# A ring of eight column copies in the token mix of a MetaFormer block, with two small instructions moved

## What is computed

```python
x = x + conv_ref(_ln_c(x), ...)         # Fourier layers, attention over the 32 tokens of a batch
t = _to_tokens(x)
t = t + ffn_ref(_ln_t(t), ...)          # a product, a batch norm, and a scan y = sigmoid(Wx + y @ V.T)
# inside conv_ref, of normed tokens:
k, q, v = (fno_layer(tokens_norm, w, skip_w, skip_b, size) for each of key, query, value)
attn = softmax(q k^T / scale) v                      # 16 heads, tokens by tokens
attn = fno_layer(attn, proj_w, proj_skip_w, ...)     # back to one channel
attn = instance_norm(attn + tokens)
m = instance_norm(attn)
m = gelu(instance_norm(spectral_conv(m, mixer_w1)) + skip1 * m)
m = instance_norm(spectral_conv(m, mixer_w2)) + skip2 * m
out = instance_norm(m) + attn
```

## Time and profile before

| | us |
|---|---|
| median of 3 runs | 428.48 (423.45 to 432.25) |
| the profiled execution | 428.99 |
| its span, first to last instruction | 427.2 |
| TensorE busy | 351.0 (82%) |
| VectorE busy | 338.9 (79%) |
| ScalarE busy | 229.8 (54%) |
| GpSimd busy | 219.3 (51%) |
| mean granted TensorE clock | 0.955 |

### The profile page before, as it was taken

One profiled execution on the slowest core, in us unless ns is written; L12 is line 12 of the kernel. 1 busy time (PEld: TensorE's weight loads), 2 busy tenths in 40 slices (PEclk: granted clock), 3 DMA queues, 4 the chain that ended last, 5 costly groups with the idle time before them and its releaser, 6 DMA issues.

```text
span 427.2 us, 7193 instructions
## 1 busy us (share of the span) xinstructions
PE 351.0 (82%) x2415; PEld 273.8 (64%) x2415; DVE 338.9 (79%) x994; ACT 229.8 (54%) x511; POOL 219.3 (51%) x265
## 2 busy tenths in 40 slices
PE   0289979998893999998999599768888889999940
PEld 0289965975451899987889558434444447767940
DVE  2999762768896958469998787999999649999990
ACT  0498851801023687445565025688776869898000
POOL 1289960041003797599961109888884779600000
PEclk9999999999998899989999869999999989999985
DMA  8999997998505000089898740222234200000997
GB/s 217 241 291 319 290 282 172 220 277 367 198 4 195 1 0 3 0 100 160 106 170 103 93 62 2 100 102 99 100 127 172 101 1 0 2 0 19 280 287 206
DMA packets 62999, 58.37 MB, mean 137 GB/s; under 512 B 5792, under 2 KB 55376, under 8 KB 60912
## 3 DMA queue, kind: packets, MB, share of 16 engines
q1 hardware_dynamic: 43232, 49.20, 38.6%
q0 software_dynamic: 16512, 8.39, 16.1%
q10 hardware_dynamic: 3216, 0.30, 0.7%
HBM read 38.84 MB, written 16.94 MB: 131 GB/s over the span
## 4 chain that ended last, share of the span: by engine, by line
PE 42%; DVE 28%; POOL 11%; issue 4%; DMA 3%; ACTq 3%; ACT 3%; SPq 2%; DVEq 0%; POOLq 0%
PE PS L640 36%; POOL BIG L571 8%; PE PS L644 6%; DVE SML L1204 6%; DVE BIG L1344 5%; DVE BIG L1536 4%; DVE BIG L1553 3%; ACTq L1007 2%; SPq L513 2%; DMA BIG<-BIG 2%; DMA BIG<-xn_rows 2%; DVE BIG L1436 1%; POOL BIG L590 1%; DVE BIG L1432 1%; POOL BIG L619 1%
## 5 line engine op out<-in xcount | busy, mean ns | idle before, releaser
L640 PE MATMUL PS<-CST,BIG 128*128 128x128 f32 (+6 forms) x994 | 123.4, 313 | 14.6 <-ACT BIG L1012 5.1
L640 PEld LDWEIGHTS PS<-CST,BIG 128*128 128x128 f32 (+1 forms) x994 | 110.9, 194 | 30.5 <-DVE BIG L1536 9.9
L1204 DVE BATCH_NORM_STATS2 SML<-BIG 128x6 f32<-128x128 f32 x256 | 53.5, 280 | 5.8 <-DMA BIG<-in_x 4.5
L640 PE MATMUL PS<-BIG 128*128 128x128 f32 (+2 forms) x450 | 53.8, 368 | 4.6 <-DVE BIG L1344 4.1
L644 PEld LDWEIGHTS PS<-CST,BIG 128*128 128x128 f32 (+1 forms) x326 | 41.4, 182 | 19.3 <-issue 13.7
L590 POOL COPY BIG<-BIG 128x512 f32<-128x512 f32 x24 | 30.5, 1320 | 39.7 <-DMA BIG<-xn_rows 36.6
L644 PE MATMUL PS<-CST,BIG 128*128 128x128 f32 (+1 forms) x326 | 48.6, 290 | 2.7 <-ACT SML L402 1.7
L640 PEld LDWEIGHTS PS<-BIG 128*128 128x128 f32 (+2 forms) x450 | 40.5, 168 | 15.4 <-issue 7.6
L640 PE MATMUL PS<-BIG,SML 128*128 128x256 f32 (+4 forms) x230 | 48.9, 415 | 0.0
L402 ACT ACTIVATE BIG<-PS 128x512 f32<-128x512 f32 (+3 forms) x59 | 32.1, 568 | 26.0 <-PE PS L640 21.0
L1577 DVE SCALAR_TENSOR_TENSOR PS<-BIG,SML,PS 128x256 f32<-128x256 f32 x92 | 41.2, 490 | 5.2 <-PE PS L640 5.1
(11 more groups left out here) (218 smaller groups left out, 496.6 us busy)
## 6 DMA issues: line engine op xcount, KB each, us to landing
xn_rows<-BIG SPq DMA_DIRECT2D x8, 1024.0 KB, 9.0
BIG<-xn_rows SPq DMA_DIRECT2D x8, 1024.0 KB, 8.8
BIG<-in_x POOLq DMA_DIRECT2D x8, 1024.0 KB, 10.9
BIG<-rs_rows SPq DMA_DIRECT2D x8, 1024.0 KB, 4.7
out_x<-BIG SPq DMA_DIRECT2D x32, 256.0 KB, 3.8
BIG<-wy_rows SPq DMA_DIRECT2D x16, 192.0 KB, 6.5
BIG<-BIG SPq DMA_DIRECT2D x16, 128.0 KB, 8.2
BIG<-in_L_conv_mixer_w SPq DMA_DIRECT2D x2, 544.0 KB, 8.9
```

The lines of the kernel that those rows point to most:

```text
L640: return pe.matmul(o, l, rhs, start=start, stop=stop, **k)
L1204: last = dve.bn_stats(ln_st[:, c % 2, row, :], src[:, XR * c + row, :])
```

## The change

The ring `x_mix` gets eight slots instead of five. It needs 4096 columns of BIG3 instead of 2560, so it begins there at column 4096 instead of 5632, and `z3_1`, which was there, goes to 14800, where `t0`, `cx` and `prob_t` have been read by then. GpSimd's first six copies no longer wait for a product; ScalarE's copy of group 7 is made ahead of its loop, and inside the loop it copies two turns ahead.

On ScalarE the square root for `al` stands ahead of the wait for `x_t` and of the first column copy. On VectorE the copy of `y_ps` to `y_m` stands behind `acft` instead of ahead of L1387.

```diff
--- before.py
+++ after.py
@@ -57,7 +57,7 @@
 LN_POOL_N = [sum(LN_POOL[:c]) // 4 for c in range(XC + 1)]
 LN_ACT_N = [4 * c - LN_POOL_N[c] for c in range(XC + 1)]
 LAG_P2, LAG_M2 = 5, 7
-MIX_RING = 5
+MIX_RING = 8
 XN_OUT = 4 * ["xn_0_3"] + 2 * ["xn_4_5"] + 2 * ["xn_6_7"]
 MIX_ACT = 4
 
@@ -268,7 +268,7 @@
             return tile[:, a:a + 1536].rearrange("p (k w h) -> p w k h", k=3, h=MH)
 
 
-        x_mix = BIG3[:, 5632:5632 + 512 * MIX_RING].rearrange("t (k w h) -> t k w h", k=MIX_RING, h=H)
+        x_mix = BIG3[:, 4096:4096 + 512 * MIX_RING].rearrange("t (k w h) -> t k w h", k=MIX_RING, h=H)
         zt = BIG3[0:64, 0:4096].rearrange("k (t p) -> k t p", p=32)
         ta1 = BIG3[:, 4096:8192].rearrange("k (g n) -> k g n", n=H)
         y_m = BIG3[:, 8192:9216]
@@ -339,7 +339,7 @@
             return a.rearrange("t (w v h) -> t w v h", v=2, h=MH)
 
 
-        z3_1 = BIG3[:, 4096:5632].rearrange("t (w k h) -> t w k h", k=3, h=MH)
+        z3_1 = BIG3[:, 14800:16336].rearrange("t (w k h) -> t w k h", k=3, h=MH)
         z3_2 = BIG3[:, 9216:10752].rearrange("t (w k h) -> t w k h", k=3, h=MH)
 
 
@@ -1071,10 +1071,11 @@
             def mix_columns(g):
                 act.activation(x_mix[:, g % MIX_RING], columns(g), ACT.Copy).then_inc(S("x_mix_act"), 1)
 
+            root(s("al"), s("rt"))
             act.wait_ge(S("xt_in"), 16 * XC)
             mix_columns(MIX_ACT - 1)
-            root(s("al"), s("rt"))
             root(s("rm"), s("rt"))
+            mix_columns(2 * MIX_ACT - 1)
 
             for g in range(32):
                 if g == 6:
@@ -1085,8 +1086,8 @@
                 act.wait_ge(S("mix_filled"), g + 1)
                 act.activation(a0[:, :, 4 * g:4 * g + 4],
                                PS[:, 4 + g % 4, :].rearrange("h (w t) -> h t w", w=4), ACT.Copy).then_inc(S("a0"), 1)
-                if g % MIX_ACT == MIX_ACT - 1 and g + MIX_ACT < 32:
-                    mix_columns(g + MIX_ACT)
+                if g % MIX_ACT == MIX_ACT - 1 and g + 2 * MIX_ACT < 32:
+                    mix_columns(g + 2 * MIX_ACT)
             load_table(ACT.Gelu)
             empty(act, "ta1", 0, 8, move_ta(ta1, 0))
             for i in range(G4 + LAG_M2):
@@ -1383,11 +1384,11 @@
             link(STT(s("va"), s("p_ma"), 2.0, s("q"), ALU.mult, ALU.add))
             inv_root(s("al"), s("va"), EPS, prm("attn_norm_g"))
             TS(dg, ident, s("al"), None, ALU.mult).then_inc(S("dg"), 1)
-            link(dve.tensor_copy(y_m, y_ps))
             link(TT(s("x0"), s("al"), s("al"), ALU.mult))
             link(TT(s("x0"), s("x0"), s("va"), ALU.mult))
             dve.wait_ge(S("bc_filled"), 1)
             TT(acft, cft, PS[:, 6, 384:512], ALU.mult).then_inc(S("acft"), 1)
+            link(dve.tensor_copy(y_m, y_ps))
             inv_root(s("rm"), s("x0"), EPS, prm("norm2_g"))
             link(TT(s("kappa"), s("rm"), prm("mixer_skip_w1"), ALU.mult))
             TS(dg, ident, s("kappa"), None, ALU.mult).then_inc(S("kap_dg"), 1)
```

## The result

| | before | after |
|---|---|---|
| median, first comparison | 425.97 (4 runs) | 433.42 (4 runs, 430.98 to 436.73) |
| ratio, 95% interval | | 1.0193 [1.0129, 1.0256] |
| median, second comparison | 426.96 (11 runs) | 434.61 (6 runs, 423.81 to 438.67) |
| the profiled execution, its span | 428.99, 427.2 | 430.98, 429.2 |

The change makes the kernel slower, by some 7 us in both comparisons. A ratio goes by those executions alone that lie within 1.5% of the fastest of their kernel; in the second comparison only one of the changed kernel's six does, so it has no ratio. The forecast was 0.7 us faster.

A forecast was written before the change was run, and what follows sets the result against it. TensorE's products were taken to lead the chain, with little room. 0.4 (start, ring and L1082 together) + 0.3 (steady) = 0.7 us less took the profiled 428.99 to 428.3 and the median 428.48 to 427.8; range 423.8 to 431.4.

The forecast's parts named there:

- What bounds the kernel: Chain that ended last: TensorE's products carry 36% of the span, the touched GpSimd line 1%, so the room is small.
- The root: ScalarE before the mix: the root for al runs 1.07 earlier, ahead of the column copy; dg comes 1.01 earlier.
- y_m and the two small products: VectorE before the mix: 1.21 removed, but L1387 and L1388 wait up to 0.98 each for copies; mix starts 0.55 earlier.
- What is late next: ScalarE's square L1082 before group 6 waits for zw, without slack; zw at 148.4 or 149.35, gain 0.8 or none.
- If GpSimd comes first: GpSimd's copy of group 8 precedes L1393: everything from there 0.95 later, zw done at 149.35.
- the four products: VectorE's L1398 to L1401 before zw: run to 145.5 if VectorE comes first, with GpSimd's copy 8 ending at 146.4.
- a clock that is low elsewhere: Listed sign that the forecast is wrong: TensorE's clock at its lower level at another place; no size given.
- The ring in the first ten groups: TensorE's two waits in the mix's first ten groups, about 0.4 + 0.3 = 0.7 us, go with eight slots.
- The steady part: Last 16 groups of the mix: 0.1145 per instruction against 0.112 free running, 0 to 0.36 to gain, 0.3 taken.
- Rival B: Late zw blocks ScalarE in front of group 6; second-norm instructions meet copies, 1.5 us slower, 430.0; chance 0.18.
- a tie at 141.04 against 141.05: VectorE's L1393 and GpSimd's copy of group 8 were forecast to start at the same moment, either possibly first.
- The chances by 2%: Whole kernel's time: faster by over 2% 0.03, slower by over 2% 0.02, within 0.95.

The follow-up runs named there:

- f4: The changed kernel once more, nothing altered: median 434.61 (6 runs), its profiled execution 423.81, the others 431.82 or more; the kernel before 426.96.
- g2: The changed kernel with ScalarE's square of zw in front of group 10 instead of 6: 425.27 (12 runs), ratio 0.9987 to the kernel before.
- g4: The changed kernel with y_m copied by ScalarE, x0's products behind acft, no GpSimd hold, the square before group 10: 427.53 (12 runs), ratio 0.9993.

## Why the prediction was wrong

*What bounds the kernel*, and that the room is small: right. No version gained more than 1.6 us in the mix.

*The root*: right, to 0.1 us. *y_m and the two small products*: right, 1.01 and 0.94 for a forecast of up to 0.98 each, the start 0.6 earlier for 0.55. Reading the port from L1199, L1385 and L1387 was sound. The Trainium skill (SBUF — State Buffer, SBUF: two separate sides) has the pair of ports held for the whole instruction by whoever starts first; the small ones bear it out. (Of L1403's 1.55 the prediction called 0.55 its own; with GpSimd held it takes 0.68.)

*What is late next*: the place was right and the size wrong, and that is the step that failed. It said "If GpSimd comes first, everything from L1393 is 0.95 later: 149.35." In the runs GpSimd did come first, and zw was done at 151.26 + 0.66 = 151.9 on the clock of the rows before: 4.2 later than the 147.75 of the rows, not 1.6. The mis-sized term is the four products. They were taken at 1.02 each in both cases, since the earlier trace rows showed a copy starved beside them for 4.11; that row shows one of two ways in which back-to-back products and copies can meet, and the other costs 0.9 after each of three products, some 2.6 us (151.9 against 149.35). Both ways fit that sentence of the Trainium skill. From zw on the prediction's own steps hold: group 10 begins 1.66 behind zw by them (the square and one eviction), which gives 152.9 on the clock of the changed kernel, and it began at 152.97. The prediction also took for granted that the order found in one profile holds in another; in one of the two profiled executions of the changed kernel zw comes within 0.03 us of the forecast, in the other 2.6 later.

A second term was missing: the sum has the clock at the start of the mix only, and nothing for a fall behind it ("a clock that is low elsewhere" stands only among the signs of being wrong). The longer wait brought one, 3.4 us at the lower level, worth 1.3 us by the 120 instructions behind it.

*The ring in the first ten groups*, 0.7 to be gained: the wait of 0.34 for GpSimd is gone in every kernel with eight slots but those with a hold; in the changed kernel it was overtaken by the 3.31 for ScalarE. *The steady part*: 168 instructions in 18.92 are 0.1126 each where TensorE doesn't wait, against 0.1145 before, so the 0.3 was there; in the changed kernel the low clock hides it. With ring and root the mix behind the first four groups takes 173.38 - 144.49 = 28.89, before 174.95 - 144.96 = 29.99: 1.1 less, where 0.7 + 0.3 was forecast. But the root alone has 28.89 as well, with five slots, so it isn't shown to be the ring's doing.

*Rival B* was the result: it named ScalarE blocked in front of group 6, and a wait of TensorE about groups 10 to 12. Of the three instructions of the second norm that it had meeting copies one did (the diagonal, 1.14; the other two took 0.16), and the products, which cost most, were not among them, so its price was 1.5 instead of 3.8, and its chance of 0.18 was too low: the text itself had found that L1082 had no slack and that zw moved the wrong way. With an order where the loser of a tie pays, no slack and a tie at 141.04 against 141.05 should have carried half of the chance.

*The chances by 2%*: 0.95 for within. The interval of the ratio is [1.0129, 1.0256], so the loss is about 2%, at the edge. The range ended at 431.4 and the median came to 433.42.

What stays open: the mix accounts for 3.8 us in the profiled pair, the medians differ by about 7. Part may be the clock: its mean is 0.927 to 0.952 in the five unprofiled executions of f4, 0.940 to 0.963 in the eleven of the kernel before beside them, and with root and y_m the fall behind the wait lasts twice as long as in the one profiled here; these five have no trace. Part is draw: in the later comparisons the kernel before had medians of 428.55, 426.96 and 427.37, 1 to 2.6 above the 425.97 of the first. Executions of one kernel differ by 9 us or more (the kernel before: 423.12 to 434.30), much of it outside the mix: the square of ma alone ends anywhere from 131.9 (root only) to 137.5 (y_m only), and whether the change adds to that was not tried. Nor was it tried what decides in an execution whether GpSimd gets its turns.

## What to carry to other kernels

Where an in-order engine does a favour between its regular duties (here the square between two evictions), its wait is a wait of everybody: put it later, as far as its own reader allows. Four groups later, 4 us of delay upstream cost TensorE nothing in g2 and 1.24 in g4, whose mix starts earlier. A wait of TensorE can also cost more than its length: 3.3 us idle here brought 1.3 more through the clock. Where VectorE and GpSimd both work from SBUF, one row of how they met is one draw; before moving anything by a microsecond, price the case in which they take turns. And an instruction moved off one path can land on another: y_m's 1.2 us went from in front of acft to in front of zw, which had no slack at all.

## What the runs showed of the hardware that was not expected

- Long VectorE instructions with both inputs in SBUF and GpSimd copies meet in two ways: GpSimd starved (copy 4.11, products 1.1) or taking turns (products 2.0). Arrivals 0.58 and 0.59 behind the start of the same product gave one and the other.
- The granted clock fell to 0.50 in the four executions in which TensorE had stood idle 3.31 to 3.88 us in the middle of the mix, and stayed at 1.00 there in the others, whose waits were 1.77 at most. It stayed low for 3.4 us once and for 6.8 three times.
- TensorE's clock came up from the lower of its two levels at different distances from the start of the mix, though it worked without a pause: 3.4 us in the kernel before, 5.3 in the execution of 423.81, and 6 in the kernel with the ring only, whose first four groups took 6.70 for 5.43. In the stretches of 1 us of the kernel with the ring only the clock is low until 146:

```profile
145.00:146.00 1.00, 1.00 (x7) 1.00 (x6) 0.96 (x2) 0.51 (x1) 1.00 (x1) 0.50 0.00 0
...
146.00:147.00 1.00, 1.00 (x11) 1.00 (x11) 1.00 (x2) 0.39 (x2) 1.00 (x2) 1.00 0.00 0
```

  That alone moves the mix by more than the change was forecast to gain (1.27 in the first four groups), and with the start at +7.00 it is more than the 1.5 by which this mix is longer than before.
